# Where eleven late dispatches and seventeen closings stand in the expert stage of a GNN and mixture-of-experts kernel

## The reference

```
x = x + gnn(layernorm(x), adj)       # agg = eps*x + adj@x; h = silu(rmsnorm(agg@W1 + b1)); h@W2 + b2
x = x + ffn(layernorm(x))            # gate -> top 2 of 8 experts, softmax of the two scores
    # each expert e: h = gelu(xf @ W1[e] + b1[e]); out += w[:, e] * (h @ W2[e] + b2[e])
```

## Time and profile before

| | |
|---|---|
| median of three runs | 490.4 us |
| the profiled execution | 493.83 us |
| its span, first to last instruction | 492.0 us |
| PE busy | 464.5 us (94%) |
| POOL busy | 299.5 us (61%) |
| granted TensorE clock, mean | 0.983 |
| chain that ended last, by engine | PE 88%, POOL 3%, issue 3%, DVE 2%, DMA 2% |

### The profile page before, as it was taken

One profiled execution on the slowest core, in us unless ns is written; L12 is line 12 of the kernel. 1 busy time (PEld: TensorE's weight loads), 2 busy tenths in 40 slices (PEclk: granted clock), 3 DMA queues, 4 the chain that ended last, 5 costly groups with the idle time before them and its releaser, 6 DMA issues.

```text
span 492.0 us, 13861 instructions
## 1 busy us (share of the span) xinstructions
PE 464.5 (94%) x3585; PEld 413.7 (84%) x3585; DVE 337.5 (69%) x1438; ACT 305.8 (62%) x942; POOL 299.5 (61%) x276
## 2 busy tenths in 40 slices
PE   8999999999999899797799999999988999999995
PEld 5687777777777568687799999999978999999995
DVE  6787788887876857475666667676556666676662
ACT  5565555666565356454566667777746777677773
POOL 3333767888786575746466566666266656666664
PEclk9999999999999989978999999999999999999998
DMA  6995333323433232333334443432245433333310
GB/s 207 376 319 144 83 93 106 83 87 82 87 86 78 67 76 71 102 95 108 99 101 123 122 136 117 116 104 72 60 124 139 125 101 103 108 102 97 94 33 12
DMA packets 50835, 54.61 MB, mean 111 GB/s; under 512 B 10249, under 2 KB 39474, under 8 KB 50760
## 3 DMA queue, kind: packets, MB, share of 16 engines
q1 hardware_dynamic: 42048, 35.14, 28.1%
q0 software_dynamic: 8240, 18.29, 10.8%
q10 hardware_dynamic: 472, 0.29, 0.2%
HBM read 33.56 MB, written 21.52 MB: 112 GB/s over the span
## 4 chain that ended last, share of the span: by engine, by line
PE 88%; issue 3%; POOL 3%; DVE 2%; DMA 2%; ACT 1%; POOLq 0%; ACTq 0%; another core or an unknown queue 0%; DVEq 0%
PE ps L748 28%; PE ps L766 27%; PE ps L654 11%; PE ps L668 10%; PE ps L741 3%; PE ps L618 3%; PE ps L661 2%; PE ps L628 2%; POOL dispatched_rows L494 1%; PE ps L635 1%; DMA vec_rows<-in_vectors 1%; ACT gelu_t L888 1%; POOL powers L483 1%; DMA eps_col<-in_epsilon 1%; PE ps L644 0%
## 5 line engine op out<-in xcount | busy, mean ns | idle before, releaser
L888 ACT ACTIVATE gelu_t<-ps,block_w 128x128 f32<-128x128 f32 x568 | 164.8, 372 | 55.4 <-PE ps L748 50.6
L766 PE MATMUL ps<-experts,gelu_t 128*128 x1136 | 153.6, 279 | 11.2 <-ACT gelu_t L888 8.6
L748 PE MATMUL ps<-slot_t,block_w 128*128 128x128 f32 x1136 | 154.1, 279 | 6.3 <-ACT gelu_t L888 4.4
L766 PEld LDWEIGHTS ps<-experts,gelu_t 128*128 128x128 f32 x1136 | 139.8, 194 | 14.8 <-issue 14.8
L748 PEld LDWEIGHTS ps<-slot_t,block_w 128*128 128x128 f32 x1136 | 140.8, 194 | 8.1 <-ACT gelu_t L888 4.9
L513 POOL DMA_INDIRECT out_y<-slot_rows x71 | 82.9, 1168 | 58.7 <-DVE slot_rows L1261 41.3
L509 POOL DMA_INDIRECT forwarded_rows<-slot_rows x71 | 81.6, 1149 | 55.0 <-DVE slot_rows L1261 47.2
L1261 DVE SCALAR_TENSOR_TENSOR slot_rows<-ps,slot_rows 128x128 f32<-128x128 f32 x133 | 46.6, 351 | 95.9 <-PE ps L766 54.3
L494 POOL DMA_INDIRECT dispatched_rows<-payload,row_idx x80 | 86.9, 1087 | 28.5 <-issue 17.6
L1152 DVE COPY block_w<-experts 128x644 f32 x142 | 70.6, 497 | 1.3 <-issue 1.3
L814 ACT ACTIVATE hidden<-ps,vec_cols 128x512 f32<-128x512 f32 x64 | 44.0, 688 | 42.0 <-PE ps L654 41.5
(11 more groups left out here) (152 smaller groups left out, 411.4 us busy)
## 6 DMA issues: line engine op xcount, KB each, us to landing
slot_rows<-forwarded_rows SPq DMA_DIRECT2D x63, 131.0 KB
slot_rows<-dispatched_rows SPq DMA_DIRECT2D x79, 67.0 KB
xs<-in_x SPq DMA_DIRECT2D x16, 256.0 KB, 6.6
xs_t<-in_x_t SPq DMA_DIRECT2D x16, 256.0 KB, 5.4
experts<-in_f_w SPq DMA_DIRECT2D x16, 256.0 KB, 4.9
slot_rows<-rrms_rows SPq DMA_DIRECT2D x13, 256.0 KB
adj_in<-in_adj_t SPq DMA_DIRECT2D x16, 128.0 KB, 5.7
dispatched_rows<-payload,row_idx POOLq DMA_INDIRECT x80
```

Source lines behind the costliest of these rows:

```text
L748: mm = pe.matmul(bank((2 * i + c // 2) % FH_BANKS, c % 2 * SLOTS, SLOTS), block_w[:, i % BLOCKS, c * P:(c + 1) * P], slot_t[:, i % 2, :], ...
L766: mm = pe.matmul(bank(Y_BANK + i % 2, 0, P), gelu_t[:, i % 2, c, :], experts[:, bass.ds(at + (OW2 + c * P), P)], start=(c == 0), stop=(c = ...
L888: act.activation(gelu_t[:, i % 2, c, :], ps[:, (2 * i + c // 2) % FH_BANKS, c % 2 * SLOTS:(c % 2 + 1) * SLOTS], ACT.Gelu, bias=block_w[:, ...
```

## The change

It moves work within POOL's and DVE's lists.

- POOL's loop over groups ends at s = 15; no dispatch of group 14 stands before write 0, and no wait for `fh_done` 6, 8, 10 or 12 is left. The eight dispatches of groups 14 and 15 stand one each behind writes 1, 4, 7, ..., 22, and the last three `second` calls behind writes 26, 29 and 32. `pow_norms(16)` stands before write 1.
- `CAUGHT_UP` is tile 87, in place of 79: tiles 71 to 87 are taken by `take_second` and closed later. From step 75 on DVE closes one tile per step, and a second one at every third step (78, 81, 84, 87), so that it catches up in step 87. PE's wait for a free PSUM bank in `layer2` follows `y_chain` for these tiles.

```diff
-        LAST_GATE, LAST_RANKS, LAST_FIRSTS = 9, 9, 11
+        LAST_GATE, LAST_RANKS = 9, 9
+        FIRSTS_BEHIND = {1 + 3 * n: (G - 2 + n // JT, n % JT) for n in range(2 * JT)}
         SECONDS_FROM = 3
+        CLOSE_FROM, CLOSE_TWICE, CAUGHT_UP = TILES + 4, 3, TILES + 16
+        SECONDS_BEHIND = {2 + 3 * (2 * JT + n): G - SECONDS_FROM + n
+                          for n in range(SECOND_GROUPS * JT - (G - SECONDS_FROM))}
...
-            for s in range(1, G + 1):
+            for s in range(1, G):
...
                 if live(s - 2):
-                    if s == G:
-                        pool.wait_ge(fh_done, 6)
                     dispatch(s - 2, 0, 0)
-                    if s == G:
-                        pow_norms(s)
-                        pool.wait_ge(fh_done, 8)
-                    elif live(s + 2):
+                    if live(s + 2):
...
             for i in range(NT):
-                if LAST_FIRSTS <= i < LAST_FIRSTS + JT:
-                    dispatch(G - 1, i - LAST_FIRSTS, 0)
-                if 0 <= (i - RING) // 4 < SECOND_GROUPS * JT - (G - SECONDS_FROM) and i % 4 == RING % 4:
-                    second(G - SECONDS_FROM + (i - RING) // 4)
+                if i == 1:
+                    pow_norms(G)
                 write_tile(i)
+                if i in FIRSTS_BEHIND:
+                    dispatch(*FIRSTS_BEHIND[i], 0)
+                if i in SECONDS_BEHIND:
+                    second(SECONDS_BEHIND[i])
...
-                if TILES <= i - 2 <= TILES + SECONDS:
+                if TILES <= i - 2 <= CAUGHT_UP:
                     pe.wait_ge(y_chain, i - 2 - TILES + 1)
...
-                if i == TILES + 4:
-                    close_second(TILES)
-                if TILES + 5 <= i <= TILES + SECONDS:
-                    close_second(2 * i - TILES - 9)
-                    close_second(2 * i - TILES - 8)
+                if CLOSE_FROM <= i <= CAUGHT_UP:
+                    n = i - CLOSE_FROM
+                    if n and n % CLOSE_TWICE == 0:
+                        close_second(TILES + n + n // CLOSE_TWICE - 1)
+                    close_second(TILES + n + n // CLOSE_TWICE)
```

More of the change, by code:

```diff
@@ L532, in _ @@
                     second(s - SECONDS_FROM)
-                if s < G:
-                    pow_norms(s)
+                pow_norms(s)
                 if s == 1:
@@ L549, in _ @@
                     dispatch(s - 2, 1, 0)
[L550 to L553, removed]
+                    pool.wait_ge(l2_done, s + 1)
                     dispatch(s - 2, 2, 0)
@@ L559, in _ @@
                     else:
-                        pool.wait_ge(fh_done, 2 if s < G else 12)
+                        pool.wait_ge(fh_done, 2)
                     dispatch(s - 2, 3, 0)
             for i in range(NT):
-                if LAST_FIRSTS <= i < LAST_FIRSTS + JT:
-                    dispatch(G - 1, i - LAST_FIRSTS, 0)
-                if 0 <= (i - RING) // 4 < SECOND_GROUPS * JT - (G - SECONDS_FROM) and i % 4 == RING % 4:
-                    second(G - SECONDS_FROM + (i - RING) // 4)
+                if i == 1:
+                    pow_norms(G)
                 write_tile(i)
+                if i in FIRSTS_BEHIND:
+                    dispatch(*FIRSTS_BEHIND[i], 0)
+                if i in SECONDS_BEHIND:
+                    second(SECONDS_BEHIND[i])
         @block.tensor
@@ L1243, in place_of_base @@
             def place_of_base(i):
-                return i if i < TILES else i - SECONDS - 1
+                return i if i < TILES else i - (CAUGHT_UP - TILES) - 1
             def bias_base(i):
@@ L1278, in has_base @@
             def has_base(i):
-                return i < TILES or TILES + SECONDS < i < NT
+                return i < TILES or CAUGHT_UP < i < NT
             bias_base(0)
@@ L1285, in _ @@
                     norm_slots(i + AHEAD)
-                if TILES < i <= TILES + SECONDS + 1:
+                if TILES < i <= CAUGHT_UP + 1:
                     dve.wait_ge(y_chain, i - TILES)
```

## The result

The changed kernel takes 496.28 us (median of six runs, 495.2 to 499.06), the kernel before, on the same chip, 490.94 us (489.8 to 492.76): ratio 1.012, interval 1.0094 to 1.0145. It is slower by about 5.3 us, where 5.2 us less had been forecast. The profiled execution took 495.98 us.

The account below looks back on a forecast made before the run. PE's early and passage stalls were taken as bound by the number and nearness of POOL's indirect DMAs. Terms 3.4 + 0 + 1.8 = 5.2 us less, from 490.4 to 485.2 us; range 474 to 494, forecast case 482 to 489 (0.38).

Parts of the forecast that it names:

- 1.83 us lie outside the span: Part of the profiled execution's 493.83 us outside the span, carried unchanged into the forecast 488.6 us.
- Later landings: Dispatches, seconds and closings landing later were to cost zero, since loads and slots need them only many tiles later.
- Groups 14 and 15, and the seconds: Early tiles: eight late dispatches become lone at 1.35 us each, 3.4 us back; three seconds stay at 1.35, nothing gained.
- The passage: From tile 71: four extra writes, one in three tiles, at 0.8 us each, 3.2 us in all, 1.8 us back.
- The zeros before the end: Moved powers, DVE's work, the dropped `fh_done` waits and later landings were each to cost nothing.
- POOL never rests: Rival: at tiles 1 to 34 and 71 to 87 short rests make extra DMAs dearer; 495.6 us at 1.9 each; slower 0.21.
- Spacing frees nearly all: Rival: a rest every third tile cuts an extra DMA's price to 0.2 us; 468 to 482 us, chance 0.28.
- The runs are not the cause: Rival: stalls come from something else at these times, so time stays at 490.4 us within a microsecond; chance 0.13.
- The late signals: Signals between PE and ACT beside runs of POOL's indirect DMAs; gelu stood up to 2.26 us behind finished PE work.
- The low clock: PE's 1.2 GHz stretch of 6.4 us early in the expert work was to vanish, clock 1.00 from 200 to 240 us.

Follow-up runs that it names:

- j2: The changed kernel itself, timed once more on the same chip as the run with the seconds as before: 495.54 us, ratio 1.0116 to before.
- e1: The changed kernel with the closings of before, so the late dispatches alone: ratio 1.0115 to before.
- e3: The changed kernel with POOL waiting at its list's end until its last two writes have landed: ratio 1.0133 to before.
- g1: The changed kernel with the powers of group 15 ahead of write 0 in place of write 1: 495.88 us, single execution.
- g4: The changed kernel with one more drain on POOL between writes 70 and 71: 492.39 us, single execution.
- h4: The changed kernel with one more drain on POOL ahead of write 126: 494.57 us, ratio 1.0061 to before.
- e2: The kernel before with the changed closings alone, late dispatches as before: ratio 0.9993 to before.
- e4: The kernel before with POOL waiting at its list's end until its last two writes have landed: ratio 1.0027 to before.
- i4: The kernel before with one more drain on POOL between writes 70 and 71: no time given, last drain 5.86 us from the last DMA.
- g2: The changed kernel with group 14's dispatches and the powers ahead of write 0, behind the fh_done waits, as before: 495.45 us, single execution.
- j1: The changed kernel with the last three second dispatches ahead of writes 16, 20 and 24 as before: 491.43 us, ratio 1.0019 to before.
- i1: The changed kernel with group 15 and the second dispatches ahead of their old writes, group 14 still spread: ratio 0.9993 to before.
- i2: The changed kernel with the last three second dispatches behind writes 24, 25 and 26: ratio 1.0046 to before.
- i3: The changed kernel with the last three second dispatches behind writes 15, 20 and 29: 504.85 us, single execution.

## Why the prediction was wrong, point by point

**The step that failed** is the end of the sum. "1.83 us lie outside the span" counts what is outside the instructions as constant, and "Later landings: [...] All zero" ends the cost of POOL's order at the last load. That between the last write and the last instruction stands a drain whose length depends on the order of 222 DMAs was not in the sum. The missing term measured +7.0 us in the profiled pair. Its row (3195 ns at 488.6) was in the trace of before: the view of line 77 would have shown that the end of the kernel waits for POOL, though only by 0.5 us (491.8 against SP's 491.3), and not that the length can change. The Trainium skill would not have led there. Its page VectorE: DVE Perf Modes, section The DRAIN you can't avoid, knows two kinds of drain, the one behind each DVE operation and one from ahead of and behind the program, constant at about 12 ns on all five engines. Of the drains of line 77 SP's, at 7 ns, would fit the second kind; ACT's, PE's and DVE's are 366 to 786 ns and POOL's 3195 to 10263, and neither kind describes them. A reader who takes them for the second is misled by up to 10 us.

**Groups 14 and 15, and the seconds (1.35 each, 3.4 us back).** Right in kind and near in size, but too small to carry a forecast. PE's turns of after, at the first long step, at a lone dispatch, and at a pair of closings, against the earlier trace rows:

```profile
202.59 0.27 PE L739 MATMUL ps<-ident,slot_n 128*128 128x128 f32 x1
...
209.02 0.42 PE L739 MATMUL ps<-ident,slot_n 128*128 128x128 f32 x1
...
222.81 0.27 PE L739 MATMUL ps<-ident,slot_n 128*128 128x128 f32 x1
...
226.09 0.27 PE L739 MATMUL ps<-ident,slot_n 128*128 128x128 f32 x1
...
362.33 0.27 PE L739 MATMUL ps<-ident,slot_n 128*128 128x128 f32 x1
...
365.76 0.27 PE L739 MATMUL ps<-ident,slot_n 128*128 128x128 f32 x1
```

The first step takes 6.43 us, 4.53 over the pace of 1.896. A pile stands beside it after all, six DMAs on POOL without a rest from 197.78 to 205.78; its first is write 1, which starts 0.20 us behind `pow_norms(16)`:

```profile
197.78 1.53 POOL L515 DMA_INDIRECT forwarded_rows<-slot_rows  x1 [0.20 <-DVE slot_rows L1259]
```

The profile of the same kernel in j2 has no such step (3.98 us is its longest there) and a pile of four. A lone dispatch at 221.34 goes with a step of 3.28 us, 1.38 over. The excess of the first 45 steps is 16.28 us for eleven extra DMAs, 1.48 each where 1.35 was forecast, against 18.22 before: 1.9 us back. One trace doesn't carry that. The seven profiles with all eleven spread (after, e1, e3, g1, g4, h4, j2) show 14.06 to 20.94, mean 16.3; the four with the old placement of all (before, e2, e4, i4) 16.73 to 19.94, mean 18.1. The 1.8 us between the means are less than the scatter of either.

**The passage (0.8 each, 1.8 us back).** Wrong. The step at 362.33 is 1.53 over, and the four pairs make 5.5 us together where 3.2 were forecast and the earlier trace rows have 5.02. From tile 78 on the new closings show a mean excess of 6.7 us in fourteen kernels (4.99 to 9.82), the old ones 6.2 in four, and e2 times at 0.9993. Spacing the closings took nothing away.

**The zeros before the end.** No run shows a cost of the powers' place (g1 ends like the changed kernel, though the pile above begins behind them), of DVE's work, of the `fh_done` waits that went (g2 likewise) or of the loads' cover. They missed one thing in the other direction: without the late write the tail from the last turn to SP's drain is 8.3 us instead of 9.9, a gain of 1.5 us that belongs to the same exchange as the loss of 7.0 (0.8 between j1 and j2).

**The sum again, with means.** 1.8 back at the dispatches, 0.5 lost at the passage, 1.5 back in the tail, 7.0 lost in the drain: 4.2 us slower, beside 5.3 timed for the whole (4.6 to 7.1 by the interval). For the seconds alone, j1 against j2, it is 7.0 lost and 0.8 back, 6.2 us, beside 4.1 timed. Neither difference is accounted for.

**The rivals.** "POOL never rests" named 495.6 us and was right in the number alone, by luck. Its price of 1.9 was not met (1.48), the expert work got no longer, and e1's slowdown goes with the drain (though its trace also has the most excess of the seven, 20.94). "Spacing frees nearly all" falls by the same price. "The runs are not the cause" is not what decided, but it comes out better than the forecast in one respect: once the drain is set aside, moving the DMAs left the time where it was (j1, e2, i1). The late signals still stand beside crowded DMAs (h4, and the six of 197.78 to 205.78), so the number of extra DMAs seems to set the price and their spacing hardly at all. Whether POOL's DMA delays the signals of others was not shown, only that they stand together. The low clock was forecast in part. In the first 60 us of the expert stage each of the four profiles with the old placement has a stretch of 6.8 us at 0.50, and the seven spread ones have none above 3.4 us (j2's clock is 1.00 throughout, after's is 0.50 from 207.9 to 211.3). No time that can be measured came of it.

## What to carry to other kernels

Before a sum is trusted, look at what every engine does behind its last useful instruction, down to the line at which the lists end: a wait put down to one engine there may be another's drain, and neither the chain of waits nor the page shows its length. In this kernel, where GpSimd issues 222 indirect DMAs, their order alone moved the last drain by 7.0 us and the time by 4.1, with none of them added; a candidate order is to be measured with the length of that drain beside the time. And a forecast of 2 to 5 us from one trace's stalls needs first the scatter of such stalls between traces, which was 3 to 7 us here.

## What the runs showed of the hardware

- POOL's drain after indirect DMAs takes 1.4 to 2.6 us for 1 to 24 of them since the drain before, 5.9 for 71, 5.1 for 120, 7.6 for 151 and 9.0 for 222, counted from the last one's end, where no late write (below) stands before it. It does so also where all of them have landed before it starts (e3: 8969 ns).
- In the kernels without a drain of their own the last one is short (1.9 to 2.0 us) just where the 114th DMA behind the last dispatch started 1.66 us late (dispatch 104: write 218; dispatch 107: write 221; none with 110 and 113, where it would be 224 and 227 of 222). The distance was forecast for i2 and i3 and held; whether that write clears anything, what, and why at that distance, stays open. A drain of one's own at a place where POOL is idle (g4, i4) takes 9.05 us there, and 71 DMAs later the last drain is 5.9 us again.
